# Extra mask multiplies on TensorE in the estimated gaps of a four-stream network kernel

## The reference

```
x = L0_attn_a_x
x = x + _L0_attn_a_ref(_layernorm(x, axis=-1), ...)   # selective scan
x = x + _L0_ffn_ref(_layernorm(x, axis=-1), ...)      # 8 experts, top 2
x = x + _L0_attn_b_ref(_layernorm(x, axis=-1), ...)   # linear attention in chunks
x = x + _L0_ffn_ref(...)
x = x + _L1_attn_a_ref(...)                           # gated linear attention
x = x + _L1_ffn_ref(...)                              # local attention, window 64, two layers
x = x + _L1_attn_b_ref(...)                           # latent attention, 16 heads
x = x + _L1_ffn_ref(...)
x = x + _L2_attn_a_ref(...)                           # scan with convolution
x = x + _L2_ffn_ref(...)                              # experts with a gate
x = x + _L2_attn_b_ref(...)                           # causal attention
x = x + _L2_ffn_ref(...)
x = x + _L3_attn_a_ref(...)                           # attention
x = x + _L3_ffn_ref(...)                              # slots
x = x + _L3_attn_b_ref(...)                           # grouped attention, global and local
x = x + _L3_ffn_ref(...)
```

## Time and profile before

| | before |
|---|---|
| median of 3 | 4017.28 us |
| profiled execution, device time | 4019.71 us |
| its span, first to last instruction | 4018.0 us |
| TensorE (PE) busy | 3198.2 us, 80% |
| VectorE (DVE) busy | 2576.6 us, 64% |
| ScalarE (ACT) busy | 2226.7 us, 55% |
| GpSimd (POOL) busy | 1506.2 us, 37% |
| mean granted clock of TensorE | 0.855 |

### The profile page before, as it was taken

How to read it: one execution, slowest core, us unless ns; L and a number is a source line. 1 busy time by engine, 2 the same in 40 slices (tenths; PEclk the granted TensorE clock), 3 DMA queues, 4 the chain that set the end, 5 groups by cost and what they waited for, 6 DMA issues and landing times. The chain is left out here.

```text
span 4018.0 us, 52382 instructions
## 1 busy us (share of the span) xinstructions
PE 3198.2 (80%) x18352; PEld 1900.7 (47%) x18352; DVE 2576.6 (64%) x6180; ACT 2226.7 (55%) x4846; POOL 1506.2 (37%) x1308
## 2 busy tenths in 40 slices
PE   3667888898888898888889767877777777889865
PEld 0234556565544554445445323655446555534422
DVE  3887875466777767566777889666443445466522
ACT  2445554345655666466656555656555565667532
POOL 2554554443445533025554555553121221122000
PEclk8787998899989999789999888889788887888755
DMA  5122222222100011200100110433313333132010
GB/s 196 42 85 78 66 72 84 78 68 67 48 1 1 1 29 51 64 13 7 45 1 1 42 39 27 136 104 101 96 49 117 96 107 102 44 91 63 13 33 12
DMA packets 193598, 238.25 MB, mean 59 GB/s; under 512 B 36984, under 2 KB 154168, under 8 KB 191288
## 3 DMA queue, kind: packets, MB, share of 16 engines
q1 hardware_dynamic: 169016, 157.43, 13.8%
q0 software_dynamic: 24320, 77.47, 6.3%
HBM read 183.61 MB, written 53.74 MB: 59 GB/s over the span
## 5 line engine op out<-in xcount | busy, mean ns | idle before, releaser
L334 ACT ACTIVATE scratch<-psum 128x512 f32<-128x512 f32 (+6 forms) x1812 | 840.3, 495 | 1017.9 <-PE psum L306 770.6
L306 PE MATMUL psum<-scratch 128*128 128x128 f32 (+14 forms) x8016 | 1008.7, 344 | 215.2 <-ACT scratch L334 45.5
L345 POOL TENSOR_TENSOR scratch<-scratch 128x512 f32<-128x512 f32 (+3 forms) x536 | 700.3, 1320 | 681.8 <-PE psum L306 237.1
L306 PEld LDWEIGHTS psum<-scratch 128*32 128x32 f32 (+8 forms) x8016 | 629.1, 155 | 611.0 <-issue 301.7
L334 ACT ACTIVATE scratch<-scratch 128x255 f32<-128x255 f32 (+9 forms) x1368 | 619.7, 480 | 473.6 <-DVE scratch L357 217.5
L306 PE MATMUL psum<-scratch,w_constants 128*128 128x512 f32 (+2 forms) x848 | 459.1, 636 | 27.2 <-ACT scratch L334 18.0
L357 DVE TENSOR_TENSOR_SCAN scratch<-scratch 128x512 f32<-128x512 f32 x256 | 420.9, 1645 | 26.3 <-POOL scratch L345 26.0
L345 DVE TENSOR_TENSOR scratch<-scratch,psum 128x512 f32<-128x512 f32 (+2 forms) x532 | 309.3, 586 | 198.1 <-PE psum L306 132.0
L310 PE MATMUL psum<-w_constants,scratch 128*128 128x128 f32 (+3 forms) x1880 | 345.3, 308 | 111.5 <-POOL scratch L345 41.5
L306 PE MATMUL psum<-scratch,w_early 128*128 128x512 f32 (+11 forms) x912 | 339.4, 518 | 99.8 <-DVE scratch L345 47.9
L365 DVE TENSOR_REDUCE scratch<-psum 128x2 f32<-128x512 f32 (+2 forms) x336 | 224.7, 677 | 223.3 <-PE psum L306 216.5
(11 more groups left out here) (104 smaller groups left out, 4149.8 us busy)
## 6 DMA issues: line engine op xcount, KB each, us to landing
scratch<-b_out SPq DMA_DIRECT2D x80, 384.0 KB
slots_out<-scratch SPq DMA_DIRECT2D x112, 128.0 KB
q_stack<-scratch SPq DMA_DIRECT2D x72, 192.0 KB
scratch<-q_out SPq DMA_DIRECT2D x96, 96.0 KB
scratch<-slots_in SPq DMA_DIRECT2D x16, 512.0 KB
q_out<-scratch SPq DMA_DIRECT2D x40, 192.0 KB
scratch<-slots_in SPq DMA_DIRECT2D x16, 448.0 KB
scratch<-q_stack SPq DMA_DIRECT2D x24, 288.0 KB
```

Of the source, the lines that this page charges most:

```text
L306: return self.engine.matmul(out, lhsT, rhs, start=start, stop=stop, **kw)
L334: return self.engine.activation(out, src, function, **kw)
L345: return self.engine.tensor_tensor(out, a, b, op)
```

## The change

The order's estimate may now put extra multiplies on PE's queue. When `Core.run` has chosen a PE program that, by the estimate, starts later than PE is free, it first looks for PE programs that wait at a yield which names banks as free (with the key of the bank's last reader). If that reader has posted by the estimate, it issues bf16 multiplies of the masks by themselves (stationary 128x128, moving 128x512) into that bank, until 60% of the gap is filled or the estimate's count of work in the stretch reaches `WANTED`. Nothing reads the results; the stream's next real multiply into the bank starts afresh. Each extra multiply waits for the bank's reader and for the masks. Some 30 yields of the PE programs now name such banks, and a few yields are added for the purpose. The multiplies count in the estimate like any other. The diff, cut to its core (five more yields in `Slots` and the one in `BlockAttention` are of the same kind):

```diff
--- before.py
+++ after.py
@@ -272,7 +272,7 @@
 
 
 
-    STEP, SPAN, ENOUGH = 30, 3413.3, 0.37
+    STEP, SPAN, ENOUGH, WANTED = 30, 3413.3, 0.37, 0.5
...
+    def keep_time(self):
+        return BANK / 2.4 / self.clock + 5
+
+    def needed(self):
+        if self.free != self.known:
+            self.at = max(self.at, self.free)
+        return self.used[int(self.free / self.SPAN)] < self.WANTED * self.SPAN
+
+    def keep_clock(self, bank, moving):
+
+        self.matmul(bank, moving[:, 0:P], moving)
...
-        self.got, self.key, self.function, self.inner = None, None, None, 0
+        self.got, self.key, self.function, self.inner, self.free_banks = None, None, None, 0, ()
...
+    LEFT = 0.4
...
-            p = best[1]
+            rank, p = best
+            if p.engine == "pe" and rank[0] > self.engines["pe"].free:
+                self.keep_clock(rank[0], going)
...
+    def keep_clock(self, until, going):
+
+        e = self.engines["pe"]
+        until -= (until - e.free) * self.LEFT
+        for p in going:
+            for bank, after in p.free_banks if p.engine == "pe" else ():
+                if any(k not in self.value or self.value[k][2] > e.free for k in (after, (0, "masks"))):
+                    continue
+                while e.free + e.keep_time() < until and e.needed():
+                    e.wait_ge(*self.value[after][:2])
+                    e.wait_ge(*self.value[0, "masks"][:2])
+                    e.keep_clock(bank, self.moving)
...
-        p.got, p.key, p.function = None, None, None
+        p.got, p.key, p.function, p.free_banks = None, None, None, ()
...
-            p.key, p.function = want
+            p.key, p.function, *p.free_banks = want
...
             e.wait_ge(*(yield self.ready))
             e.matmul(self.one, self.center, self.src).then_inc(*b.post("centred", tag))
+            e.wait_ge(*(yield b["squares", tag], None, (b.b, self.ready)))
         e.wait_ge(*(yield b["squares", tag]))
         e.matmul(self.two, self.mean, self.sq).then_inc(*b.post("variance", tag))
+        e.wait_ge(*(yield b["normed", tag], None, (b.b, b["norm", "logvar", tag])))
...
+                e.wait_ge(*(yield self["squares", name], None, (self.b, self["norm", "logvar", "x" if name == "q" else "q"])))
...
-        e.wait_ge(*(yield self["silu", "v"]))
+        e.wait_ge(*(yield self["silu", "v"], None, (self.b, self["norm", "logvar", "k"])))
...
-        e.wait_ge(*(yield self["gated"]))
+        e.wait_ge(*(yield self["gated"], None, (self.b, self["norm", "logvar", "o"])))
...
-    def pe_route(self, e, n):
+    def pe_route(self, e, n, turn_read):
...
-        e.wait_ge(*(yield self["router", "kept"]))
+        e.wait_ge(*(yield self["router", "kept"], None, (self.b, turn_read)))
...
-            e.wait_ge(*(yield self["rows", g // 2, "x"]))
+            e.wait_ge(*(yield self["rows", g // 2, "x"], None, *(((self.b, b_free), (self.a, self["router", "beyond"])) if g == 0 else ())))
...
-        e.wait_ge(*(yield self["router", "mixed"]))
+        e.wait_ge(*(yield self["router", "mixed"], None, (self.a, self["biased", self.BLOCKS - 1])))
...
-        e.wait_ge(*(yield self["router", "mixed"]))
+        e.wait_ge(*(yield self["router", "mixed"], None, (self.b, self["glu", self.BLOCKS - 1])))
...
-                e.wait_ge(*(yield self["full", before]))
+                e.wait_ge(*(yield self["full", before], None, (self.b, self["normed", "x"])))
...
-        e.wait_ge(*(yield self["v_all"]))
-        e.wait_ge(*(yield self["parts", "g"]))
+        e.wait_ge(*(yield self["v_all"], None, (self.b, self["normed", "x"])))
+        e.wait_ge(*(yield self["parts", "g"], None, (self.b, self["normed", "x"])))
...
-        e.wait_ge(*(yield self["rows", 0, 0]))
+        e.wait_ge(*(yield self["rows", 0, 0], None, (self.a, self["token", "v_tok"]), (self.b, self["parts", "rest", 1])))
...
-            e.wait_ge(*(yield self["rows", bt, kind, "rows"]))
+            e.wait_ge(*(yield self["rows", bt, kind, "rows"], None, *((() if bt else ((self.a, self["rope", kind, "logs"]), (self.b, self["rope", kind, "logs"]))))))
...
-        e.wait_ge(*(yield self["slot", "hT"]))
+        e.wait_ge(*(yield self["slot", "hT"], None, (self.b, self["slot", "hidden_bias"])))
...
-        e.wait_ge(*(yield self["row", "scaled", "alpha"]))
+        e.wait_ge(*(yield self["row", "scaled", "alpha"], None, (self.a, self["slot", "x_tok"]), (self.b, self["slot", "raw_logits"])))
...
-        e.wait_ge(*(yield self["slot", "new"]))
+        e.wait_ge(*(yield self["slot", "new"], None, (self.a, self["gate", "parts"]), (self.b, self["gate", "parts"])))
...
         bf16_masks = Weights(ctx.enter_context(nc.sbuf_tensor("bf16_masks", [P, n], BF16)), where["masks"])
+        core.moving = bf16_masks.buf[:, 0:BANK]
```

More of the change, by code:

```diff
@@ L1223, in pe @@
         n = self.hidden
-        yield from self.pe_route(e, self.L + self.E)
+        yield from self.pe_route(e, self.L + self.E, self["token", "x"])
         yield from self.pe_blocks(e, self["token", "x"])
@@ L1346, in pe @@
     def pe(self, e):
-        yield from self.pe_route(e, self.E)
+        yield from self.pe_route(e, self.E, self["router", "tokens"])
         yield from self.pe_blocks(e, self["router", "tokens"])
@@ L1460, in pe @@
             if before:
-                e.wait_ge(*(yield self["full", before]))
+                e.wait_ge(*(yield self["full", before], None, (self.b, self["normed", "x"])))
             e.matmul(self.a[0:3 * K, :], w[f"w{c}"], self.xn).then_inc(*self.post("proj", c))
-        e.wait_ge(*(yield self["full", "g"]))
+        e.wait_ge(*(yield self["full", "g"], None, (self.b, self["normed", "x"])))
         e.matmul(self.a, w["wv"], self.xn).then_inc(*self.post("proj", "v"))
-        e.wait_ge(*(yield self["v_all"]))
-        e.wait_ge(*(yield self["parts", "g"]))
+        e.wait_ge(*(yield self["v_all"], None, (self.b, self["normed", "x"])))
+        e.wait_ge(*(yield self["parts", "g"], None, (self.b, self["normed", "x"])))
         for i in range(n):
@@ L2809, in pe @@
         last.then_inc(*self.post("slot", "sums"))
-        e.wait_ge(*(yield self["slot", "input"]))
+        e.wait_ge(*(yield self["slot", "input"], None, (self.b, self["slot", "denominator"])))
         for i in range(3):
@@ L2825, in pe @@
         last.then_inc(*self.post("slot", "scores"))
-        e.wait_ge(*(yield self["slot", "p"]))
+        e.wait_ge(*(yield self["slot", "p"], None, (self.a, self["slot", "exp"])))
         e.wait_ge(*(yield self["slot", "v"]))
@@ L2830, in pe @@
         last.then_inc(*self.post("slot", "p_turned"))
-        e.wait_ge(*(yield self["slot", "pt"]))
+        e.wait_ge(*(yield self["slot", "pt"], None, (self.a, self["slot", "exp"])))
         for bt in range(B):
@@ L2843, in pe @@
         e.wait_ge(*(yield self["slot", "read_v"]))
-        e.wait_ge(*(yield self["slot", "alpha_t"]))
+        e.wait_ge(*(yield self["slot", "alpha_t"], None, (self.a, self["slot", "read_v"])))
         for bt in range(B):
@@ L2848, in pe @@
         last.then_inc(*self.post("slot", "read"))
-        e.wait_ge(*(yield self["slot", "read_out"]))
+        e.wait_ge(*(yield self["slot", "read_out"], None, (self.b, self["slot", "alpha_t"])))
         e.matmul(self.b, w["wo"], self.xn).then_inc(*self.post("out"))
```

## The result

The changed kernel takes 3840.84 us (median, 3832.93 to 3841.05), the kernel before 4020.23 us beside it on the same chip. The ratio is 0.955, 95% interval 0.9533 to 0.9568: 180 us faster, where 27 were forecast.

A forecast was written before the change was run, and what follows sets the result against it. It took four dependent chains sharing one in-order PE queue as the bound, with PE's own latency a good part of each. Clock gain -44 us plus 17 us cost, reordering 0, made -27 us: 3990 us, range 3940 to 4040.

The forecast's parts named there:

- The direction and the mechanism of the multiplies: Extra multiplies in PE's idle gaps raise the clock and shorten the run; this case had chance 0.60, 3945 to 4012 us.
- The forecast of their cost: On PE's queue, one multiply in five of 450 stands in the way, 0.35 us each, 0.55 on path: 17 us.
- A different order moves waits about: On every queue, the estimate's counting of multiplies may change the order, either sign: 0, bounds 25 us each way.
- My rival of the order: The new order loses more than the gain, time 4040 us; chance 0.07.
- The amount turned: Over PE's span, 186 us of filled gaps turn 264 us from low to high clock, bounds 100 and 450.
- The price of a us turned: Each us turned to the high clock saves 0.30 us of PE, x 0.55 on the path: 0.165 us.
- My 44 us gained: Gain from the higher PE clock: 264 us turned x 0.165 = 44 us, bounds 16 and 74.
- upper bound of 74 us: Largest gain allowed from the higher PE clock, with 450 us turned, before any cost of the multiplies.
- PE's share of the path: PE taken as 0.55 of the path everywhere, down from 6/10 in the chain traced over the last tenth.
- the factor of 1.75: PE's same forms at low against high clock: 594 against 1141 ns, 275 against 446 ns, taken as 1.75.
- the sum of my terms: Whole kernel: -44 us from the clock, +17 us for multiplies in the way, reordering 0: -27 us.

The follow-up runs named there:

- short version: Changed kernel with its 643 extra multiplies cut from 512 to 8 moving columns, same order and waits: 0.9805 of the kernel before, clock 0.872.
- second dose: Changed kernel's order with each extra multiply issued twice (1286): 0.9605 of the kernel before, 3875.7 us against 3860.4 for the changed kernel on that chip.
- order alone: Changed kernel's order and estimate, with no extra multiply or its waits issued: 0.980 of the kernel before, on another chip 0.977 (3929.7 us).
- fourth set: On one chip: changed kernel 0.956, its order without multiplies 0.977, kernel before's order with uncounted multiplies 0.989, changed kernel with estimate's semaphore latency 75 0.9545.
- add-only run: Kernel before's order on every queue, extra multiplies issued but not counted in the estimate: 0.9865 of the kernel before, on another chip 0.989 (3982.3 us).
- high-clock order: Kernel before with an estimate that always reckons with the high clock, no extra multiplies: 0.992 of the kernel before, clock 0.866.
- order with 70: Kernel before, estimate's semaphore latency 70 instead of 80: 0.975, again 0.977 (3917.8 us); with uncounted multiplies added 0.965 (3867.1 us).
- order with 81: Kernel before with the estimate's semaphore latency 81 instead of 80, no extra multiplies: 0.984 of the kernel before.
- changed kernel with 82: Changed kernel with the estimate's semaphore latency 82 instead of 80, multiplies issued: 0.985 of the kernel before, clock 0.899.
- first set: On one chip (kernel before 3951 us): changed order without multiplies 0.980, old order with uncounted multiplies 0.9865, changed kernel with 8-column multiplies 0.9805.

## Why the prediction was wrong, step by step

**The direction and the mechanism of the multiplies: right.** The multiplies lift the clock (0.863 to 0.911 within one order), f32 work gets shorter from the kernel before to the changed one (the first group of the page from 344 to 327 ns, the w_early group from 518 to 473), PE's idle time shrinks and ACT and DVE wait less for PE in all. The forecast of their cost (17 us, 0.04 us each) isn't contradicted: nothing measurable for the queue slots and waits (short version), 0.04 to 0.06 us for each of a second dose. What the first 643 cost in themselves no run shows.

**"A different order moves waits about; ... I give it 0 with bounds of 25 us each way": the step that failed.** The order alone is worth 90 us in the fourth set. It turns only some 93 us to the high clock there (median clock 0.852 to 0.861), which at 0.2 us each is 19 us, so most of its worth isn't the clock. I took the reordering for a disturbance of a few waits. It also decides what is left over at the end: 149 us alone at the low clock before, 23 us with the new order and no multiply. The trace of the add-only run, in the old order, leaves it alone for 147 us, that of the high-clock order for 113, that of the order with 70 for 64. But the order with 81 leaves it alone for 178 us and is still 1.6% faster than the kernel before, since its other three streams end early (the third at 3792 us, against 3867). So the lonely end is one part of what an order costs, how early the first three end is another, and how the order's 90 us divide between them was not shown, since no run changed the end alone. The order of the kernel before is the slowest of the five orders that were timed without multiplies (1, 0.992, 0.984, 0.977 and 0.975 to 0.977), so a gain from a new order was likelier than a loss. It was not certain: the changed kernel with 82 stands at 0.985 with its multiplies, and if they are worth there what they are elsewhere, its order by itself is hardly better than that of the kernel before. How the two kernels stood could have been read from the estimate: of the 21 settings of the semaphore latency from 70 to 90, the kernel before has the fourth latest end (3756 us, of 3626 to 3779) and the changed kernel the fifth earliest (3577 us, of 3538 to 3717). The two ends lie 179 us apart; that this meets the 180 us measured is in part luck, since the estimate is some 260 us short of either time and reckons with a clock of its own. There was a sign in the trace too: the last 118 us at PE busy 49% and a clock of 0.50 I read as a stretch to be warmed, and not as a stretch that need not be there. My rival of the order had only the bad sign.

**The amount turned: too small, within the bounds.** I said 264 us, bounds 100 and 450. By the medians of the clocks and spans of all executions of a set, the multiplies turn 412 us in the changed kernel's order, 322 us in the order with 70, and 344 and 360 us in the old order (fourth set, 0.852 to 0.894; first set, 0.863 to 0.908). The core lists above, of one execution each, give 391 us for the first and 328 for the second. The whole change turned 505 us on the fourth set's chip, so the other 93 are the order's. The number of multiplies, 643, was within 200 to 900, with 450 said.

**The price of a us turned: too low, the second term that failed.** Net of the multiplies' own cost it is 85/412 = 0.21 us in the new order, 51/322 = 0.16 in the order with 70, and 37/344 = 0.11 and 56/360 = 0.15 in the old one. My 44 us gained less 17 us paid over 264 us was 0.10 net. Adding 0.04 us for each of the 643 (or 732) back, the gross price is 0.27 and 0.25 in the two better orders and 0.19 and 0.24 in the old one, against my 0.165. With more us turned, at a higher price, the multiplies gained 85 us net in the new order where I had 27, and that is above even my upper bound of 74 us before costs; without the order's 90 us the changed kernel would still stand near 3932 us, just below my range. I had taken PE's share of the path from the last tenth of the chain, which runs nearly alone; that the middle depends more on PE, since each late result holds several streams, would explain it, but no run tests that. One reading behind the factor of 1.75 was also loose: the 275 ns are of multiplies and the 446 ns of transposes. It did no harm, since 128-column transposes in the window of the earlier trace rows have a median of 272 ns.

In the old order the sum of my terms, 27 us, is not far from the 37 to 56 measured. The forecast of 3990 us was that of the multiplies without the order, against 3982 us measured for just that in the fourth set; the first set's ratio, 0.9865, makes it 3963.

**What stays open.** Why the multiplies are worth 85 us in the order made with them and 37 to 56 us in the others. These cases differ in two ways at once, in the order and in whether the estimate counted the multiplies when it placed them. Where the estimate counts them, its gaps lie nearer to the real ones; that would be a cause, but it was not tested. Nor was it tested whether the last stream can be helped on purpose: only chance orders were tried.

## What to carry to other kernels

Multiplies with unread results can pay where a stream waits, the bank is free and the engine's clock falls with idleness: here 0.1 to 0.2 us net for each us that leaves the low clock, with no measurable cost for their queue slots and waits and an estimated 0.04 to 0.06 us for each beyond what the gaps hold. But in a kernel whose order comes from an estimate, an edit of the estimate is two changes. Time the new order without the new work, and the new work in the old order, and disturb the order by a constant that means nothing: here that alone moved the time by 2.5%, more than the multiplies did. Read where the estimate's own account ends, too, before and after the edit and with a few meaningless settings: here it told the poor orders of each kernel from the good ones. Look at how the streams end, too: one stream alone for 149 us is a sign of an order that can be bettered, though not a measure of it.

## What was not expected of the hardware

The kernel before took 3951 us on one chip and 4015 to 4029 us on the others, 1.6 to 2.0% apart, which no run here explains, while the ratio of the same edits repeats (order alone 0.980 and 0.977, multiplies alone 0.9865 and 0.989). The program with the multiplies alone shows 624 of them in one trace and 732 in another, so records were missing from the first; the weight loads are complete, 19084 in both. Of the changed kernel's 643 one trace shows 523, again with the full 18995 weight loads. The count of such a group of multiplies is a lower bound, and the weight loads tell the number. The second trace's group:

```profile
L516 PE MATMUL psum<-bf_masks 128*128 128x512 bf16 x732 | 228.0, 431 | 15.5 <-DVE scratch L358 10.3 <-ACT scratch L347 3.6 <-DVE scratch L382 1.3
```
